# Gate and up of the last layer by Strassen's method, two batches at a time

## The chip, the core and the metric

The kernel runs on one core of a Trainium2 chip (trn2). The metric is the device time of one execution in microseconds (us). A program on this core has five instruction streams that run side by side and wait for each other by semaphores: TensorE (PE in the profile, its weight loads PEld), VectorE (DVE), ScalarE (ACT), GpSimd (POOL) and SyncE (SP), which here issues the loads and stores.

## The reference

Four sublayers on x of 4 batches x 512 tokens x 512 features, float32: attention over a context, a mixture of experts, a second attention, and a feed-forward layer, which alone is changed:

```python
x = fwht(x * SU_ug) / SCALE
x_up = x @ W_up.T * (Wscale_ug[:INTER] * SCALE)
x_gate = x @ W_gate.T * (Wscale_ug[INTER:] * SCALE)
x = jax.nn.silu(x_gate) * x_up
x = fwht(x * SU_dp) / SCALE
x = x @ W_down.T * (Wscale_dp * SCALE)
```

Its input is the layernorm of the running x, its output is added to it; INTER is 2048. fwht is a Hadamard transform over the last axis.

## The kernel before

A matrix product in this kernel is three: every operand is split into a high and a low part of TensorE's rounded fp32 type, ACT copying the high part and DVE subtracting it from the raw value, and `product` (L91) multiplies high by high, high by low and low by high into one PSUM bank. The last layer is `final_ffn` (L2887). The transforms of its hidden side are folded into the down weights ahead of it (`fold_dram`). It has 64 steps `s`, `divmod(s, NF)` being the batch b and the tile j of 128 of the 2048 hidden features. Per step, TensorE computes gate and up of the tile for the 512 tokens of the batch (`gate_up`, 2 x 4 x 3 matmuls of 512 columns), always one step ahead, and then `down`, 4 x 3 matmuls that add to four PSUM banks psY over the 16 tiles of a batch. ACT applies silu, DVE multiplies by up and its scale, casts the high part and subtracts for the low (`hidden`), and both split the next weights. After the last tile of a batch DVE adds the four banks to x (`add_y`) and SP stores it. The order of each stream is the one in which its loop is written.

The layer's input for the next batch is made beside that: DVE's statistics (`stats`, four rows at j = 1), GpSimd's `rstd`, then for each 128 tokens ACT's `row_norm`, GpSimd's `row_fly` (five instructions: the signs and two butterfly levels), TensorE's `turn_row` (transposes) and `rotate` (a product with a Hadamard matrix of 128), each result split by ACT and DVE. Turns and rotations are put between gate and up of the next step and the down product (`beside`), in banks that gate and up need two steps later. Loads of gate and up (512 KB) and down (256 KB) are three steps ahead, in slots of one buffer (`final_raw`).

## Time and profile before

| | us |
|---|---|
| median of 3 runs | 2234.42 |
| lowest and highest | 2230.71, 2235.13 |
| the profiled execution | 2232.4 |
| its span, first to last instruction | 2230.6 |
| busy in the span: PE, PEld | 2205.2, 1844.6 |
| DVE, ACT, POOL | 1436.4, 1043.1, 470.0 |

Busy times are those of one profiled execution, on the same scale as its span. A matmul's record reaches into the next one's, so busy PE time is that of overlapping records; what one takes from the stream is the distance of two starts. The mean granted clock of TensorE is 0.999 of full speed.

### The profile page before, as it was taken

To read this page: it belongs to the slowest core of one execution; us is meant where nothing else is said; L and a number is where in the kernel's file an instruction comes from. 1 tells how busy PE (TensorE), PEld (TensorE's weight loads), DVE (VectorE), ACT (ScalarE), POOL (GpSimd) and SP (SyncE) were. 2 spreads that over 40 slices of the span, in tenths; PEclk is the share of its full clock that TensorE was granted. 3 is DMA by queue.
4 is the path that set the end of the run, shared out by engine and by line. 5 is a ranking of instruction groups with operands and counts; after the bars stand their busy time and mean duration, and the time that the engine had idled before them with its cause. 6 is when DMAs were issued, how large, how long until landed. Compare 5 with 4: busy or idle time off the path is not lost. (4 is left out here: it accounts for less than half of the span.)

```text
span 2230.6 us, 32169 instructions
## 1 busy us (share of the span) xinstructions
PE 2205.2 (99%) x11065; PEld 1844.6 (83%) x11065; DVE 1436.4 (64%) x2993; ACT 1043.1 (47%) x1871; POOL 470.0 (21%) x445
## 2 busy tenths in 40 slices
PE   8999999999999999999999999999999999999999
PEld 6778788888999977888888888888878888888887
DVE  7864365546777766777777777777776555555544
ACT  5532220114556566666666666666664233223221
POOL 4432545521111171011000010000142102121000
PEclk9999999999999999999999999999999999999999
...
DMA packets 92171, 219.58 MB, mean 98 GB/s; under 512 B 9568, under 2 KB 30560, under 8 KB 89248
## 3 DMA queue, kind: packets, MB, share of 16 engines
...
q8 instruction: 65, 1.06, 0.2%
...
## 5 line engine op out<-in xcount | busy, mean ns | idle before, releaser
L2245 ACT ACTIVATE route_weights<-route_weights,xa_minus_max 128x512 f32<-128x512 f32 x256 | 184.7, 722 | 188.6 <-DVE xa_minus_max L2400 188.5
L2416 DVE TENSOR_TENSOR xa_late_hi<-xa_ps_t,route_wv_hi 128x512 fp32r<-128x512 f32 x256 | 174.8, 683 | 118.3 <-ACT route_wv_hi L2254 118.1
L2183 POOL TENSOR_TENSOR route_kv_lo<-route_rows,route_kv_hi 128x1024 fp32r<-128x1024 f32 x32 | 77.0, 2407 | 695.2 <-ACT route_kv_hi L2219 695.2
L2254 ACT ACTIVATE route_wv_hi<-xa_ps_t 128x512 fp32r<-128x512 f32 x256 | 151.1, 591 | 93.7 <-PE xa_ps_t L2606 66.7
L2400 DVE CUSTOM_DVE_ANT_0 route_weights<-xa_ps_s,route_mask_bias 128x512 f32<-128x512 f32 x256 | 175.5, 686 | 0.6 <-issue 0.6
L2992 ACT ACTIVATE ffn_silu<-ffn_ps_gate,late_scales 128x512 f32<-128x512 f32 x63 | 43.5, 690 | 244.7 <-PE ffn_ps_gate L96 244.7
L2606 PEld LDWEIGHTS xa_ps_t<-ident,route_weights 128*128 128x128 f32 x1024 | 126.5, 140 | 36.4 <-issue 3.8
L2606 PE MATMUL xa_ps_t<-ident,route_weights 128*128 128x128 f32 x1024 | 153.3, 272 | 1.9 <-DVE xa_late_hi L2416 1.8
L94 PE MATMUL xa_ps_p<-route_wv_hi,route_kv_hi 128*128 128x512 f32 x288 | 119.2, 414 | 3.0 <-PEq L1632 1.4
L2798 DVE TENSOR_TENSOR route_kv_lo<-route_weights,route_kv_hi 128x1024 fp32r<-128x1024 f32 x42 | 53.8, 1282 | 99.7 <-ACT route_kv_hi L2793 99.7
L1095 ACT ACTIVATE moe_silu<-moe_ps_gate 128x512 f32<-128x512 f32 x44 | 26.3, 597 | 190.3 <-PE moe_ps_gate L96 190.3
L94 PE MATMUL xa_ps_p<-late_xT_hi,late_wq_hi 128*128 128x512 f32 (+1 forms) x264 | 113.6, 430 | 0.2 <-DVE late_wq_lo L2798 0.2
L96 PE MATMUL xa_ps_p<-route_wv_hi,route_kv_lo 128*128 128x512 f32 x288 | 113.2, 393 | 0.0
L94 PE MATMUL xa_ps_s<-route_kv_hi,xa_q_hi 128*128 128x512 f32 x256 | 103.6, 405 | 0.7 <-DVE xa_minus_max L2400 0.7
L94 PE MATMUL xa_ps_o<-route_first_lo,xa_late_lo 128*128 128x512 f32 x256 | 103.5, 404 | 0.0
L96 PE MATMUL xa_ps_p<-late_xT_hi,late_wq_lo 128*128 128x512 f32 (+1 forms) x264 | 103.4, 392 | 0.0
L95 PE MATMUL xa_ps_p<-late_xT_lo,late_wq_hi 128*128 128x512 f32 (+1 forms) x264 | 102.6, 389 | 0.0
L2422 DVE TENSOR_TENSOR x<-xa_ps_o,x 128x512 f32<-128x512 f32 x126 | 86.1, 683 | 25.5 <-PE xa_ps_o L96 24.4
L94 PE MATMUL ex_ps_h<-ex_xT_hi,ex_w_hi 128*128 128x256 f32 (+1 forms) x360 | 101.9, 283 | 0.4 <-DVE ex_w_lo L1758 0.4
L96 PE MATMUL ex_ps_h<-ex_xT_hi,ex_w_lo 128*128 128x256 f32 (+1 forms) x360 | 101.1, 281 | 0.0
L96 PE MATMUL xa_ps_s<-route_kv_hi,xa_q_lo 128*128 128x512 f32 x256 | 100.7, 393 | 0.0
L94 PE MATMUL ffn_ps_y<-ffn_down_hi,ffn_hidden_hi 128*128 128x512 f32 x256 | 100.3, 392 | 0.0
...
## 6 DMA issues: line engine op xcount, KB each, us to landing
...
```

What stands on the lines that cost most here:

```text
L94: pe.matmul(out, lh, rh, start=start, stop=False)
L95: pe.matmul(out, lh, rl, start=False, stop=False)
L96: return pe.matmul(out, ll, rh, start=False, stop=stop)
L2183: pool.tensor_tensor(kvl[b % 2][:], rawkv[b % 2], f32(kvh[b % 2][:]), ALU.subtract).then_inc(M.kv_ready, 1)
L2245: act.activation(prob[slot][:], prob[slot][:], ACT.Exp, bias=nmx[:, slot:slot + 1], scale=-1.0, accum_out=tot[:, slot:slot + 1]).then_inc( ...
L2254: act.activation(PTh[:, :, tt * P:(tt + 1) * P], psT[tt % 2][:].rearrange("p (k n) -> p k n", k=TT), ACT.Copy).then_inc(M.pt_hi, 1)
L2400: dve.tensor_tensor_reduce(out=prob[slot][:], in0=psS[slot % 2][:], in1=maskb[:, b * S:(b + 1) * S], scale=-SCALE, scalar=3.4e38, op0=ALU. ...
L2416: dve.tensor_tensor(PTl[:, :, tt * P:(tt + 1) * P], psT[tt % 2][:].rearrange("p (k n) -> p k n", k=TT), f32(PTh[:, :, tt * P:(tt + 1) * P] ...
L2422: dve.tensor_tensor(x[:, t, :], psO[tt % 2][:], x[:, t, :], ALU.add).then_inc(M.x_added, 1)
L2606: last = pe.transpose(psT[tt % 2][:, k * P:(k + 1) * P], prob[tt][:, k * P:(k + 1) * P], ident)
L2798: dve.tensor_tensor(L.gu_lo[s % 3][:], final_raw(G, s)[0], f32(L.gu_hi[s % 3][:]), ALU.subtract).then_inc(L.gu_ready, 1)
L2992: act.activation(hid[s % 2][:], gate[:], ACT.Silu, scale=gate_s[:, j:j + 1]).then_inc(M.silu_done, 1)
```

## The change

Batches 0 and 1 form a pair, and 2 and 3. The gate and up weights of a tile are taken as a 2 x 2 matrix of blocks (gate or up by half of the 512 inputs), the inputs of a pair as another (half of the inputs by batch). Seven products of blocks, P1 to P7, replace eight; each block product is 2 x 3 matmuls. Their operands are sums of blocks: `weight_sums` makes those of the weights in place on GpSimd, for every tile anew, and DVE and ACT split them beside the plain weights; t1 to t4, of the inputs, are made once per pair of batches, t1 and t2 by DVE, t3 and t4 by GpSimd, from unsplit copies (`rot_copy`) that ACT writes beside the split ones. The products are added up in SBUF: five additions on DVE, two on GpSimd, copies of P1 and P5 on ACT. The first batch's hidden tile goes on to its down product as before; the second's is kept, unsplit, in one of seven places, and its down products are done in flushes after tiles 5, 10 and 15 (10 and 15 in the first pair), since psY holds one batch at a time; each change of batch adds psY to x. The first five tiles of the first pair are plain steps of batch 0, and later of batch 1, while the inputs of batch 1 are not all there. So there are 37 steps, 10 plain and 27 of pairs, and 64 down products. Transposes and rotations move to other steps; rotations come after the down product. Rows 4 and 5 and unsplit copies for batch 0 are made in the attention before. Gate and up weights have two split slots instead of three.

```diff
+PLAIN = 5
+KEPT = 7
+PAIR_BATCHES = ((0, 1), (2, 3))
+FLUSH = ((10, NF - 1), (5, 10, NF - 1))
...
+def final_steps():
+    steps = []
+    for p, (a, b) in enumerate(PAIR_BATCHES):
+        plain = 0 if p else PLAIN
+        steps += [Step("plain", p, j, a) for j in range(plain)]
+        kept = []
+        for j in range(plain, NF):
+            kept.append(len(steps))
+            steps.append(Step("pair", p, j, a))
+            if j in FLUSH[p] and not (plain and j == NF - 1):
+                steps[-1].tail, kept = kept, []
+        steps += [Step("plain", p, j, b) for j in range(plain)]
+        if kept:
+            steps[-1].tail = kept
+    return steps
...
-        NORM1, TURN1, NORM2, ROT1, TURN2, ROT2 = 2, 6, 7, 8, 10, 12
+        TURNS = {0: (4,), 1: (5,), 2: (6, 7), 15: (8, 9), 16: (10,), 17: (11,), 18: (12, 13), 19: (14,), 20: (15,)}
+        ROTATES = {1: 2, 2: 3, 17: 4, 18: 5, 19: 6, 20: 7}
+        NORMS = {1: (6,), 2: (7,), 9: (8,), 10: (9,), 16: (10, 11), 17: (12,), 18: (13,), 19: (14, 15)}
+        STATS = {6: 2, 8: 3}
...
+                def weight_sums(s):
+                    pool.wait_ge(L.gu_ready, splits_before(s) + 1)
+                    q = [final_raw(G, s)[0][:, i * 2 * P:(i + 1) * 2 * P] for i in range(4)]
+                    sums.link(pool.tensor_tensor(q[3], q[2], q[3], ALU.add))
+                    sums.link(pool.tensor_tensor(q[2], q[0], q[2], ALU.subtract))
+                    sums.link(pool.tensor_tensor(q[0], q[3], q[0], ALU.subtract))
+                    pool.tensor_tensor(q[1], q[1], q[0], ALU.subtract).then_inc(M.sums_taken, 1)
+                def t3(p):
+                    pool.wait_ge(M.t_odd, 2 * p + 1)
+                    if p == 0:
+                        pool.wait_ge(M.x_lo, x_count(p, "b1"))
+                    pool.tensor_tensor(X.raw_t3, X.raw_b[1], X.raw_b[0], ALU.subtract).then_inc(M.t_even, 1)
+                def t4(p):
+                    pool.wait_ge(M.t_odd, 2 * p + 2)
+                    pool.tensor_tensor(X.raw_t4, X.raw_a[1], X.raw_t2, ALU.subtract).then_inc(M.t_even, 1)
+                def add_p5(q):
+                    pool.wait_ge(M.p5_copied, q + 1)
+                    pool.wait_ge(M.added, added_count(q, "p1_p6"))
+                    if q:
+                        pool.wait_ge(M.kept_ready, q)
+                    pool.tensor_tensor(part[2], part[0], kept[q % KEPT], ALU.add).then_inc(M.p5_added, 1)
+                    pool.wait_ge(M.added, added_count(q, "p1_p6_p7"))
+                    pool.tensor_tensor(kept[q % KEPT], part[0], kept[q % KEPT], ALU.add).then_inc(M.p5_added, 1)
+                for s in range(NSTEPS):
+                    if is_pair(s + 1):
+                        weight_sums(s + 1)
+                    if is_pair(s):
+                        add_p5(STEPS[s].pairs)
+                    if s in (PLAIN - 1, LAST_PLAIN):
+                        t3(STEPS[s + 1].pair)
+                        t4(STEPS[s + 1].pair)
+                    if s in STATS:
+                        rstd(STATS[s])
+                    for t in NORMS.get(s, ()):
                         row_fly(pool, L, t)
 
...
+                    else:
+                        if opens:
+                            x_high(st.pair, "t3")
+                        split_gate_up(s + 1)
...
+                        act.wait_ge(M.product_done, product_count(q, "p5"))
+                        act.activation(kept[q % KEPT], bank_p5[:], ACT.Copy).then_inc(M.p5_copied, 1)
+                        if not (opens or followed):
+                            hidden_high(s - 1)
+                        act.wait_ge(M.product_done, product_count(q, "p1"))
+                        if opens:
+                            act.wait_ge(M.hidden_ready, s)
+                        act.activation(part[0], bank_p1[:], ACT.Copy).then_inc(M.p1_copied, 1)
+                        if not (opens and STEPS[s - 1].tail):
+                            split_down(STEPS[s - 1].event + 1)
+                        act.wait_ge(M.added, added_count(q, "gate_a"))
+                        silu(s, 1, part[1])
+                        if opens:
+                            x_high(st.pair, "t4")
+                        if tail:
+                            tail_high(s - 1, 0)
+                        split_sums(s + 1)
+                        act.wait_ge(M.added, added_count(q, "gate_b"))
+                        silu(s, 2, part[2])
+                        if tail:
+                            hidden_high(s)
+                        for e in range(len(tail)):
+                            split_down(STEPS[s - 1].event + 2 + e)
+                            tail_high(s - 1, e + 1)
+                    for t in NORMS.get(s, ()):
+                        row_norm(act, G, L, t)
...
+                def keep(s):
+                    j, q = STEPS[s].j, STEPS[s].pairs
+                    dve.wait_ge(M.silu_done, s + q + 2)
+                    dve.wait_ge(M.p5_added, 2 * q + 2)
+                    tile = kept[q % KEPT]
+                    dve.scalar_tensor_tensor(out=tile, in0=tile, scalar=up_s[:, j:j + 1], in1=part[2],
+                                             op0=ALU.mult, op1=ALU.mult).then_inc(M.kept_ready, 1)
+                def gate_a(q):
+                    dve.wait_ge(M.product_done, product_count(q, "p2"))
+                    dve.wait_ge(M.p1_copied, q + 1)
+                    dve.wait_ge(M.hidden_ready, pair_step(q))
+                    dve.tensor_tensor(part[1], bank_p2[:], part[0], ALU.add).then_inc(M.added, 1)
...
+                def seventh(q):
+                    dve.wait_ge(M.product_done, product_count(q, "p7"))
+                    dve.wait_ge(M.p5_added, 2 * q + 1)
+                    dve.tensor_tensor(part[0], bank_p7[:], part[0], ALU.add).then_inc(M.added, 1)
...
+                def up_a(q):
+                    dve.wait_ge(M.step_done, pair_step(q) + 1)
+                    dve.wait_ge(M.p5_added, 2 * q + 2)
+                    dve.tensor_tensor(part[0], bank_p4[:], part[0], ALU.add).then_inc(M.added, 1)
...
+                    else:
+                        if opens:
+                            x_low(st.pair, "t3")
+                        split_gate_up(s + 1)
+                        gate_a(q)
+                        sixth(q)
+                        if not (opens and STEPS[s - 1].tail):
+                            split_down(STEPS[s - 1].event + 1)
+                        seventh(q)
+                        if opens:
+                            x_low(st.pair, "t4")
+                        if tail:
+                            tail_low(s - 1, 0)
+                            add_y(STEPS[s - 1].event)
                         else:
+                            split_sums(s + 1)
+                            if opens:
+                                add_y(STEPS[s].event - 1)
+                        gate_b(q)
+                        up_a(q)
+                        hidden(s, 1, part[0])
+                        for e in range(len(tail)):
+                            split_down(STEPS[s - 1].event + 2 + e)
+                            tail_low(s - 1, e + 1)
+                            if e == 0:
+                                split_sums(s + 1)
+                        if tail:
+                            add_y(st.event - 1)
+                    if s in STATS:
+                        for t in range(STATS[s] * TT, STATS[s] * TT + TT):
                             stats(t)
...
+                add_y(STEPS[-1].event)
+                split_down(STEPS[-1].event + 1)
+                for e in range(len(STEPS[-1].tail)):
+                    tail_low(NSTEPS - 1, e)
+                    split_down(STEPS[-1].event + 2 + e)
...
+                def pair_up(s, between):
+                    st = STEPS[s]
+                    q, p = st.pairs, st.pair
+                    w, sums = (L.gu_hi[s % 2], L.gu_lo[s % 2]), (sum_hi[s % 2], sum_lo[s % 2])
+                    opens = not is_pair(s - 1)
+                    pe.wait_ge(L.gu_ready, splits_before(s) + 2)
+                    if opens:
+                        pe.wait_ge(M.prod_done, s - 1)
+                        pe.wait_ge(M.x_lo, x_count(p, "t1"))
+                    else:
+                        pe.wait_ge(M.p5_copied, q)
+                        pe.wait_ge(M.added, added_count(q - 1, "p1_p6_p7"))
+                    times(bank_p5, sums, 3, X.t1).then_inc(M.product_done, 1)
+                    times(bank_p1, w, 0, X.a[0]).then_inc(M.product_done, 1)
+                    if opens:
+                        pe.wait_ge(M.silu_done, s + q)
+                    else:
+                        pe.wait_ge(M.added, added_count(q - 1, "gate_b"))
+                    times(bank_p2, w, 1, X.a[1]).then_inc(M.product_done, 1)
+                    if opens:
+                        pe.wait_ge(M.prod_done, s)
+                        pe.wait_ge(M.x_lo, x_count(p, "t2"))
+                    else:
+                        pe.wait_ge(M.added, added_count(q - 1, "up_a"))
+                    times(bank_p6, sums, 0, X.t2).then_inc(M.product_done, 1)
+                    between(range(TT // 2))
+                    if opens:
+                        pe.wait_ge(M.x_lo, x_count(p, "t3"))
+                    pe.wait_ge(M.p1_copied, q + 1)
+                    times(bank_p7, sums, 2, X.t3).then_inc(M.product_done, 1)
+                    between(range(TT // 2, TT))
+                    pe.wait_ge(M.added, added_count(q, "gate_a"))
+                    times(bank_p3, sums, 1, X.b[1]).then_inc(M.product_done, 1)
+                    if opens:
+                        pe.wait_ge(M.x_lo, x_count(p, "t4"))
+                    pe.wait_ge(M.added, added_count(q, "p1_p6"))
+                    times(bank_p4, w, 3, X.t4).then_inc(M.step_done, 1)
...
+                for s, st in enumerate(STEPS):
+                    if s == LAST_PLAIN:
+                        turns(s)
+                        down_step(s)
+                        rotates(s)
+                        for r in st.tail[:-1]:
+                            down_kept(r)
+                        pair_up(s + 1, lambda tiles: down_kept(st.tail[-1], tiles))
+                    elif is_pair(s + 1):
+                        pair_up(s + 1, lambda tiles: down_step(s, tiles))
+                        for r in st.tail:
+                            down_kept(r)
```

In the order of the instructions, VectorE first: one step of a tile before (`ffn_silu` is the hidden tile, `route_kv` and `late_wq` the gate and up weights), and one pair step of the change (`ffn_part` are sums of products, `ffn_sums` the weight sums, `route_rows` here a kept tile). The semaphores in brackets bear names of earlier sublayers, whose numbers they reuse.

```order
L2798 TENSOR_TENSOR late_wq_lo<-route_weights,late_wq_hi 128x1024 [waits late_gate_up_hi]
L3041 SCALAR_TENSOR_TENSOR ffn_silu1<-ffn_ps_up1,late_scales,ffn_silu1 128x512 [waits ca_x_loaded0,ca_x_loaded1]
L3046 CAST ffn_hidden_hi1<-ffn_silu1 128x512 [waits ca_ln_xT_ready]
L3048 TENSOR_TENSOR ffn_hidden_lo1<-ffn_silu1,ffn_hidden_hi1 128x512 [waits ca_ln_hi_ready]
L3014 TENSOR_TENSOR ffn_down_lo2<-route_weights,ffn_down_hi2 128x512 [waits ca_ctx_loaded0]
```

```order
L2897 TENSOR_TENSOR route_kv_lo0<-route_weights,route_kv_hi0 128x1024 [waits late_gate_up_hi]
L3417 TENSOR_TENSOR ffn_part1<-ffn_ps_gate0,ffn_part0 128x512 [waits ca_ln_pool_chain,ca_ln_chain,ca_ln_stats_done]
L3423 TENSOR_TENSOR ffn_part0<-ffn_ps_up0,ffn_part0 128x512 [waits moe_table_taken,ca_ln_stats_done]
L3333 TENSOR_TENSOR ffn_down_lo2<-route_weights,ffn_down_hi2 128x512 [waits ca_x_loaded3]
L3429 TENSOR_TENSOR ffn_part0<-ffn_ps_up1,ffn_part0 128x512 [waits moe_table_summed,ca_ln_stats_done]
L3343 TENSOR_TENSOR route_kv_lo1<-route_weights,route_kv_hi1 128x1024 [waits late_gate_up_hi]
L3434 TENSOR_TENSOR route_wv_room_5188<-ffn_ps_gate0,route_wv_room_5188 128x512 [waits moe_table_summed,ca_ln_stats_done]
L3439 TENSOR_TENSOR ffn_part0<-ffn_ps_up0,ffn_part0 128x512 [waits moe_table_summed,ca_ln_hi_ready]
L3392 SCALAR_TENSOR_TENSOR ffn_part1<-ffn_part0,late_scales,ffn_part1 128x512 [waits ca_ln_xn_turned,moe_table_taken]
L3410 SCALAR_TENSOR_TENSOR route_rows<-route_rows,late_scales,route_wv_room_5188 128x512 [waits moe_table_summed,ca_ln_xn_turned]
L3402 TENSOR_TENSOR ffn_hidden_lo0<-ffn_part1,ffn_hidden_hi0 128x512 [waits ca_ln_rstd_ready]
```

Five instructions for one tile of one batch have become eleven for one tile of two.

GpSimd, which before has nothing in a step but, at some, the rows of the next batch (no row of it names a weight or a product): its part of a pair step, the four sums of weights and the two additions of a product.

```order
L3146 TENSOR_TENSOR route_weights<-route_weights 128x256 [waits late_gate_up_ready]
L3147 TENSOR_TENSOR route_weights<-route_weights 128x256 [waits ca_x_loaded0]
L3148 TENSOR_TENSOR route_weights<-route_weights 128x256 [waits ca_x_loaded0]
L3149 TENSOR_TENSOR route_weights<-route_weights 128x256 [waits ca_x_loaded0]
L3168 TENSOR_TENSOR route_wv_room_5188<-ffn_part0,route_rows 128x512 [waits moe_hot_ready,moe_table_taken,ca_first]
L3170 TENSOR_TENSOR route_rows<-ffn_part0,route_rows 128x512 [waits moe_table_taken]
```

The sums wait for VectorE's split of the plain weights, which they overwrite; the additions wait for VectorE's and VectorE's next for them.

VectorE in the step after tile 10 of the first pair, where batch 1's kept tiles are multiplied: after the addition of P7, from the split of the first kept tile to that of the second (`route_first_lo` and `mask_room` take the split tiles).

```order
L3367 TENSOR_TENSOR route_first_lo<-route_rows,route_first_lo 128x512 [waits moe_counts_ready]
L3378 TENSOR_TENSOR x<-ffn_ps_y0,x 128x512 [waits moe_routed]
L3378 TENSOR_TENSOR x<-ffn_ps_y1,x 128x512 [waits moe_routed]
L3378 TENSOR_TENSOR x<-ffn_ps_y2,x 128x512 [waits moe_routed]
L3378 TENSOR_TENSOR x<-ffn_ps_y3,x 128x512 [waits moe_counted]
L3434 TENSOR_TENSOR route_wv_room_5188<-ffn_ps_gate0,route_wv_room_5188 128x512 [waits moe_table_summed,ca_ln_stats_done]
L3439 TENSOR_TENSOR ffn_part0<-ffn_ps_up0,ffn_part0 128x512 [waits moe_table_summed,ca_ln_hi_ready]
L3392 SCALAR_TENSOR_TENSOR ffn_part1<-ffn_part0,late_scales,ffn_part1 128x512 [waits ca_ln_xn_turned,moe_table_taken]
L3410 SCALAR_TENSOR_TENSOR route_wv_room_5188<-route_wv_room_5188,late_scales 128x512 [waits moe_table_summed,ca_ln_xn_turned]
L3402 TENSOR_TENSOR ffn_hidden_lo1<-ffn_part1,ffn_hidden_hi1 128x512 [waits ca_ln_rstd_ready]
L3333 TENSOR_TENSOR ffn_down_lo0<-route_weights,ffn_down_hi0 128x512 [waits ca_x_loaded3]
L3367 TENSOR_TENSOR mask_room_5187<-route_rows,mask_room_5187 128x512 [waits moe_counts_ready]
```

Four additions to x and the rest of the pair step now stand between the split of the first kept tile and that of the second.

## Rows read from the trace of the kernel before

**Rows 1.** The page: busy time, share of the span and instructions
```profile
PE 2205.2 (99%) x11065; PEld 1844.6 (83%) x11065; DVE 1436.4 (64%) x2993; ACT 1043.1 (47%) x1871; POOL 470.0 (21%) x445
```

**Rows 2.** Waits of PE from 1690 us: total, times, longest
```profile
PE ffn_ps_up L94 <- PEq L2119: 0.6, 1, 0.6
```

**Rows 3.** Stretches of the last layer: length, busy by engine, PEclk, DMA share, GB/s
```profile
1965.00:2096.00 131.00, 131.00 (x595) 108.95 (x594) 74.27 (x100) 39.15 (x57) 23.54 (x24) 1.00 0.30 100
2096.00:2227.00 131.00, 131.00 (x579) 108.48 (x578) 58.86 (x84) 32.05 (x45) 0.00 (x0) 1.00 0.25 81
```

**Rows 4.** Timeline of PE and ACT: start, length, engine, line, operation
```profile
1992.29 0.39 PE L94 MATMUL ffn_ps_gate<-late_xT_hi,late_wq_hi 128*128 128x512 f32 x1
...
1997.73 0.39 PE L94 MATMUL ffn_ps_y<-ffn_down_hi,ffn_hidden_hi 128*128 128x512 f32 x1
...
2210.73 0.39 PE L96 MATMUL ffn_ps_gate<-late_xT_hi,route_kv_lo 128*128 128x512 f32 x1
...
2211.15 0.69 ACT L2992 ACTIVATE ffn_silu<-ffn_ps_gate,late_scales 128x512 f32<-128x512 f32 x1 [6.00 <-PE ffn_ps_gate L96]
```

**Rows 5.** Timeline of DVE while POOL is idle
```profile
1821.74 1.23 DVE L2798 TENSOR_TENSOR route_kv_lo<-route_weights,route_kv_hi 128x1024 fp32r<-128x1024 f32 x1 [4.48 <-ACT route_kv_hi L2793]
1822.89 0.75 DVE L3041 SCALAR_TENSOR_TENSOR ffn_silu<-ffn_ps_up,late_scales,ffn_silu 128x512 f32<-128x512 f32 x1
1823.67 0.43 DVE L3046 CAST ffn_hidden_hi<-ffn_silu 128x512 fp32r<-128x512 f32 x1
1824.13 0.69 DVE L3048 TENSOR_TENSOR ffn_hidden_lo<-ffn_silu,ffn_hidden_hi 128x512 fp32r<-128x512 f32 x1
1824.74 0.69 DVE L3014 TENSOR_TENSOR ffn_down_lo<-route_weights,ffn_down_hi 128x512 fp32r<-128x512 f32 x1
```

**Rows 6.** Timeline of DVE at the end
```profile
2225.43 2.73 DVE L3035 TENSOR_TENSOR x<-ffn_ps_y,x 128x512 f32<-128x512 f32 x4 [1.46 <-PE ffn_ps_y L96]
```

**Rows 7.** Groups of ACT from 1700 us: busy, mean ns, idle before
```profile
L2992 ACT ACTIVATE ffn_silu<-ffn_ps_gate,late_scales 128x512 f32<-128x512 f32 x63 | 43.5, 690 | 244.7 <-PE ffn_ps_gate L96 244.7
L2793 ACT ACTIVATE route_kv_hi<-route_weights 128x1024 fp32r<-128x1024 f32 x41 | 43.3, 1055 | 1.4 <-DMA route_weights<-in_ffn_w 1.4
L2982 ACT ACTIVATE ffn_down_hi<-route_weights 128x512 fp32r<-128x512 f32 x63 | 39.4, 625 | 0.0
```

**Rows 8.** Timeline of DVE, then POOL, around a row of the next batch
```profile
1762.45 1.76 DVE L2798 TENSOR_TENSOR route_kv_lo<-route_weights,route_kv_hi 128x1024 fp32r<-128x1024 f32 x1
1764.13 0.74 DVE L3041 SCALAR_TENSOR_TENSOR ffn_silu<-ffn_ps_up,late_scales,ffn_silu 128x512 f32<-128x512 f32 x1
1764.90 1.55 DVE L3046 CAST ffn_hidden_hi<-ffn_silu 128x512 fp32r<-128x512 f32 x1
...
1764.89 1.29 POOL L2817 TENSOR_TENSOR late_rows<-late_rows 128x512 f32<-128x512 f32 x1
1766.26 0.80 POOL L2821 TENSOR_TENSOR late_rows<-late_rows 128x256 f32<-128x256 f32 x1
...
1768.28 0.74 POOL L2821 TENSOR_TENSOR late_rows<-late_rows 128x256 f32<-128x256 f32 x1
```

**Rows 9.** Groups of POOL from 1600 us
```profile
L2821 POOL TENSOR_TENSOR late_rows<-late_rows 128x256 f32<-128x256 f32 x32 | 28.8, 900 | 2.5
...
L2183 POOL TENSOR_TENSOR route_kv_lo<-route_rows,route_kv_hi 128x1024 fp32r<-128x1024 f32 x2 | 4.8, 2410 | 24.0 <-ACT route_kv_hi L2219 24.0
```

**Rows 10.** Timeline of DVE, then POOL: statistics of one batch
```profile
1841.66 0.69 DVE L152 BATCH_NORM_STATS2 late_ln_stats<-x 128x6 f32<-128x512 f32 x1
...
1844.76 0.18 DVE L154 BATCH_NORM_AGGREGATE late_ln_mean_var<-late_ln_stats 128x2 f32<-128x6 f32 x1
...
1845.11 0.23 POOL L135 TENSOR_SCALAR late_ln_var_eps<-late_ln_mean_var 128x4 f32<-128x4 f32 x1 [75.39 <-DVE late_ln_mean_var L154]
...
1847.60 0.24 POOL L140 TENSOR_SCALAR late_ln_shift<-late_ln_shift 128x4 f32<-128x4 f32 x1
```

**Rows 11.** Waits of PE over the whole span, the longest in total
```profile
PE xa_ps_t L182 <- DVE late_xT_lo L171: 2.6, 2, 2.0
```

589 lines of the change are left out of this document (430 added, 159 removed).

## The prediction

> **What bounds the kernel now.** I read the shares of busy time first, then the waits of TensorE in the last layer, then the durations of what stands in its loops. TensorE (PE) is busy 99% of the span [rows 1]. From 1690 us to the end it waited once, 0.6 us at the start of the stage [rows 2], and in the stretches from 1965 to 2227 us it is busy all the time at clock 1.00, while VectorE (DVE) has 74 and 59 of each 131 us and GpSimd (POOL) 24 and 0 [rows 3]. So the last layer is as long as its matmuls. A removed matmul is worth its pitch, not its listed 0.39 us, since records overlap: the 24 of one gate and up start at 1992.29 and the next product at 1997.73 [rows 4], 5.44 / 24 = **0.2267 us**. Six take 1.36, twelve 2.72. A result is seen by others 0.19 us after its pitch ends: last start 2210.73, ScalarE (ACT) starts at 2211.15 [rows 4].
>
> The excerpts of the order show the method in force: a step for a pair of tiles has seven block products of six matmuls instead of eight. 27 pairs save 27 x 6 = 162 matmuls, **36.7 us**. The down products stay. Everything else in the change either lies beside TensorE or makes it wait; all of the prediction is in how long it waits, since now it never does.
>
> **Prices.** DVE with both inputs in SBUF: 1.23 us for 128x1024, 0.69 for 128x512 (back to back 1.15 and 0.61 apart) [rows 5]. The multiplication by the scale takes 0.75 [rows 5], an addition of a product from PSUM 2.73 / 4 = 0.68 [rows 6]. ACT: 1.06 for 1024 columns, 0.62 for 512, silu 0.69 [rows 7]. GpSimd: 0.74 for 256 columns and 0.08 to the next that needs it, 1.29 for 512 [rows 8], 2.41 for 1024 [rows 9].
>
> **Two engines that shut each other out.** In [rows 8] GpSimd's row work runs beside DVE's splits. The cast that takes 0.43 alone [rows 5] takes 1.55: GpSimd started 0.01 us before it and ran 1.29, to 1766.18, and 1.29 + 0.43 is about what is seen, a wait to the end of the other's instruction. A split of 1.23 takes 1.76 there. The multiplication in between, one input of which is in PSUM, takes 0.74 as ever. So I count: of the new DVE work, what has both inputs in SBUF takes turns with GpSimd, instruction by instruction; what reads a product from PSUM doesn't. The Trainium skill, SBUF — State Buffer (on the ports shared by VectorE and GpSimd), calls it an exclusive lock held for a whole instruction. [...]
>
> **The loop of a pair step.** TensorE's own time is (42 + 12) x 0.2267 = 12.24. Let T be the start of P5. The first order excerpt lists DVE's eleven instructions, the second GpSimd's six. In the steady state the sums are ready at T. Then GpSimd's second addition (1.29, after DVE's split of the sums) T+1.3; up_a T+2.0; the product of the first batch T+2.75; that kept for the second T+3.5; hidden_lo (ACT's hi beside it) T+4.2; the split of the next gate and up T+5.4; GpSimd's four sums 4 x 0.82 = 3.3, with DVE's split of down (0.6) in between, T+9.4; its first addition T+10.7; DVE's seventh T+11.4 and the split of the sums, T+12.7. So the loop is about **12.75**: TensorE waits 0.5 per step once no slack is left. Slack comes where TensorE is late for another reason: then hidden_lo ends at T+3.1 (P4, 0.19, up_a, 0.75, 0.75, 0.69), and three steps pass free. Over both halves I count 3.6 us of such waits (0 if the loop is 12.0; 12 if it is 13.2).
>
> **What is put into that loop has no cover.**
> - Statistics of batches 2 and 3, at steps 6 and 8: 3.3 us on DVE (from 1841.66 to 1844.94) and 2.7 on GpSimd before the next sums [rows 10], of which 1.8 count behind the split: next sums at T+17, 4.8 late. Twice: **9.6** (6 to 11).
> - Rows 8 and 9 on GpSimd at steps 9 and 10: 1.29 + 4 x 0.74 + gaps = 4.4, taking turns with four DVE instructions. Sums at T+16.6, 4.4 late; the other one falls in a flush and makes it 4.0 longer: **8.4** (0 to 10).
> - Flush inside a run of pairs, three times (third order excerpt). The second kept tile needs from DVE, from T+10.7 on: seventh, a split, four additions to x, gate_b, up_a, two products, hidden_lo, a split of down, a split: thirteen instructions, 9.1 us, T+19.8. TensorE is there at T+12.24+2.72 = 14.96, so it waits 4.85. 3 x 4.85 = **14.6** (9 to 17; 3 each if seventh is not held up by GpSimd).
> - The end: after the last P4 nothing is left to cover up_a, the product, ACT's hi and hidden_lo: 0.19 + 0.68 + 0.75 + 0.62 + 0.69 and gaps, 3.15. Then the first kept tile is split only behind four additions to x that wait for the last down product: 2.25. **5.4** (4 to 7). The finish behind it, the additions to x [rows 6] and the stores, stays.
>
> **Openings.** Let C be the end of gate and up of step 3. The rotation of batch 1's last rows is copied at C+5.2. Then in DVE's order: t1 1.2, three splits 3.6, gate and up 1.2 (C+11.2); GpSimd's sums 3.9, ACT 1.06, and DVE waits for GpSimd's 2.4 of t3 to end before its split: C+18.7. TensorE, after gate and up of step 4 and a down product, stands from C+13.4: 5.3. Behind it t2, hidden of step 4 (its cast waits for GpSimd's t4) and the split of t2 end at C+24.7, P6 waits 1.9; t4 makes P4 wait 2.7 and the next sums 1.1. **11.0** (6 to 14; 5.6 without turns). The second opening, after step 20, is alike but with five kept tiles in between: GpSimd has rows 14 and 15 (8.8 us from about 4.6 before the end of gate and up of step 20) ahead of the sums; ACT's split of these stands ahead of row 15's; the rotation waits 4.7 and row 15 1.0; t3 holds the second kept tile back 3.1; x4, the sums and the additions to x behind them cost 1.3 + 1.2 + 2.6. **14** (6 to 18).
>
> **Rotations.** At steps 1, 2, 17 and 18 they now come after the down product, into the bank that gate and up of the step after next needs at once: TensorE waits 0.9 for two ACT copies (0.19 + 0.62 + the rest of the first). **3.6** (2 to 6). The copies and rows moved ahead into the attention are on ACT and GpSimd, whose waits there end with TensorE; 0, up to 2 if that cover is gone. The additions to x grow from 16 to 40; those in the flush are in the sum, the others lie beside kept products. Loads keep their bytes, 768 KB each 8 us before, and less each step now: 0.
>
> **Sum.** Waits 3.6 + 9.6 + 8.4 + 14.6 + 5.4 + 11.0 + 14 + 3.6 = 70.2; less 36.7 is +33.5. The profiled execution took 2232.4 (span 2230.6), 2.0 under the median of 2234.4. 2232.4 + 33.5 = **2266**, and its own range, with errors of a few us in each wait, 2250 to 2282.
>
> **Rivals.**
> 1. *The loop fits (faster).* Place: the sums' split against the next P5. If the engines did not take turns, the loop loses 0.6 + 1.2 and is 10.9; if DVE's order also leaves room for statistics, rows and second opening, only rotations 3.6, first opening 5.6, flush 3 x 3 and end 5.4 remain, 23.6: 2232.4 - 36.7 + 23.6 = **2219**. It decides when all waits are under 36.7. For it: DVE's own work in a step is 8.4 of 12.24 us, GpSimd's 5.9. Against: they are in one chain, and the stretched rows [rows 8]. 0.12.
> 2. *No turns, but the chain as I have it.* Statistics 6.2 and second opening 6 on top: 35.8 of waits, **2231.5**, no change to be told. 0.12, half of it within 0.2%.
> 3. *Waits that cost more.* GpSimd's in-place sums at the 0.90 mean of [rows 9] instead of 0.74 make the loop 0.6 longer, some 9 us over about 15 steps without slack. Or the clock: no wait in this kernel is over 2.0 us [rows 11] and the clock of the last layer stays 1.00 [rows 3]; here nine are over 3. At the lower level, 1.2 GHz, a block product is 1.36 longer; one after each wait is 12.2. **2278**. The Trainium skill, TensorE: Matmul & The Clock Gate (on the gate), says that an idle engine is put to half rate and comes back after sustained work; no row here shows it. 0.14.
>
> The forecast has 0.62. A measurement of this kernel can tell 0.2%, 4.5 us, from no change. Faster: 0.12 + 0.02; same: 0.06; slower: 0.62 + 0.14 + 0.04 = 0.80. The range reaches from rival 2 to past rival 3: 2231 to 2286 leaves out rival 1 and a little above.
>
> **What would show it.** 2142 matmuls of 512 columns in the last layer; PE busy well under all of the time between 1704 us and the end. The longest waits: P5 of steps 5, 8, 10 and 11 for DVE's split of the sums; a down product for the split of a kept tile in three flushes, 4 to 9 us; the rotation of step 20. DVE's SBUF splits over their 1.23 and 0.69 in the mean, the additions from PSUM at 0.68. It is wrong if P5 to P5 is 12.3 in plain pair steps with the sums ready well ahead, if the splits are not stretched, or if GpSimd's additions end before P7 does.

## The result and the profile after

The changed kernel takes **2282.5 us** in the median of 4 runs (2280.8 to 2284.3), the kernel before, on the same chip, 2233.3 (2230.7 to 2235.1). The ratio is **1.022, interval 1.021 to 1.024: slower**. The profiled execution took 2282.8 with a span of 2281.0 us, 50.4 more than the 2230.6 of before. The forecast was 2266 with a range to 2286, so direction and range held; the place of half of the loss did not.

Shares of busy time and the granted clock in 40 slices of the changed kernel:

```profile
PE 2195.0 (96%) x10903; PEld 1826.5 (80%) x10903; DVE 1522.1 (67%) x3103; ACT 1125.6 (49%) x1996; POOL 660.1 (29%) x611
...
PEclk9999999999999999999999999999999999999999
```

Against [rows 1], TensorE has 162 matmuls less and is busy 10 us less, not 36.7: part of the busy time is matmuls at a lower clock. The row of PEclk shows nothing at one digit; the mean granted clock of the span is 0.988 against 0.999.

TensorE's waits from 1690 us (us in total, times, longest), where the kernel before had the one of [rows 2]:

```profile
PE ffn_ps_up L94 <- PEq L2122: 12.9, 1, 12.9
PE ffn_ps_gate L94 <- DVE ffn_sums_lo L3343: 8.9, 4, 4.0
PE ffn_ps_y L94 <- DVE route_first_lo L3367: 7.7, 3, 2.9
PE ffn_ps_gate L94 <- DVE route_kv_lo L3343: 6.4, 3, 4.3
PE ffn_ps_gate L2931 <- POOL late_rows L2922: 3.4, 1, 3.4
PE ffn_ps_y L94 <- DVE ffn_hidden_lo L3402: 3.4, 2, 3.0
...
PE ffn_ps_y L94 <- DVE x L3378: 2.9, 1, 2.9
```

One line was not in the forecast at all: 12.9 us for "PEq", TensorE's own sequencer. It is the boundary between the block of the attention and that of the last layer. Timelines there, of TensorE, GpSimd and ScalarE:

```profile
1697.71 0.39 PE L96 MATMUL xa_ps_o<-route_first_lo,xa_late_lo 128*128 128x512 f32 x1
1710.98 0.77 PE L94 MATMUL ffn_ps_up<-late_xT_hi,late_wq_hi 128*128 128x512 f32 x1 [12.88 <-PEq L2122]
...
1697.44 0.24 POOL L140 TENSOR_SCALAR late_ln_shift<-late_ln_shift 128x4 f32<-128x4 f32 x1
1698.61 1.26 POOL L2916 TENSOR_TENSOR late_rows<-late_rows 128x512 f32<-128x512 f32 x1 [0.93 <-ACT late_rows L2904]
...
1706.41 0.72 POOL L2922 TENSOR_TENSOR late_rows<-late_rows 128x256 f32<-128x256 f32 x1
...
1697.71 1.52 ACT L2904 ACTIVATE late_rows<-x,late_ln_shift,late_ln_rstd 128x512 f32<-128x512 f32 x2 [6.12 <-POOL late_ln_shift L140]
1710.65 0.63 ACT L3192 ACTIVATE ffn_down_hi<-route_weights 128x512 fp32r<-128x512 f32 x1 [11.42 <-PEq L2122]
```

TensorE's last product of the attention starts at 1697.71. GpSimd then still has rows 4 and 5 ahead of it, ten instructions to 1707.13, and no engine passes into the next block before it: ScalarE starts there at 1710.65, TensorE at 1710.98.

The rest of the waits, 45.8 us in 26 places, lie where the forecast had put them, mostly smaller. And the clock, in stretches of 20 us (length, busy and matmuls of TensorE, granted clock, DMA share, GB/s):

```profile
1710.00:1730.00 20.00, 19.02 (x75) 0.85 0.44 158
1750.00:1770.00 20.00, 15.69 (x62) 0.91 0.14 41
...
1790.00:1810.00 20.00, 15.98 (x65) 0.91 0.19 64
1830.00:1850.00 20.00, 15.71 (x61) 0.91 0.15 52
...
2130.00:2150.00 20.00, 20.00 (x90) 1.00 0.23 59
```

and the two us behind the wait for P5 of step 8, first as such a stretch, then in the timeline of TensorE, a block product of six:

```profile
1806.00:1808.00 2.00, 2.00 (x6) 0.50 0.60 195
...
1805.45 0.80 PE L94 MATMUL ffn_ps_gate<-late_xT_hi,ffn_sums_hi 128*128 128x512 f32 x1 [4.02 <-DVE ffn_sums_lo L3343]
1806.04 0.63 PE L95 MATMUL ffn_ps_gate<-late_xT_lo,ffn_sums_hi 128*128 128x512 f32 x1
1806.47 0.63 PE L96 MATMUL ffn_ps_gate<-late_xT_hi,ffn_sums_lo 128*128 128x512 f32 x1
...
1807.75 0.63 PE L96 MATMUL ffn_ps_gate<-late_xT_hi,ffn_sums_lo 128*128 128x512 f32 x1
1808.17 0.47 PE L94 MATMUL ffn_ps_up<-late_xT_hi,late_wq_hi 128*128 128x512 f32 x1
1808.48 0.40 PE L95 MATMUL ffn_ps_up<-late_xT_lo,late_wq_hi 128*128 128x512 f32 x1
```

Between 1806.04 and 1807.75 the matmuls start 0.43 us apart, at a granted clock of 0.50, which is 1.2 GHz; from 1808.48 they are back at the 0.2267 of [rows 4]. [Rows 3] had no stretch under 1.00.

**Where 50.4 us come from.** I went through TensorE's timeline from start to start of its records and counted what lies over 0.2267 us a record. Behind the boundary that is 72.4 us more than in the same stage of the kernel before: 45.8 of listed waits; 15.6 in 78 matmuls that start 0.40 to 0.43 apart; and 11.0 in what stands beside the waits, since the record before a wait and the first one behind it last longer, about 0.4 us together. The boundary costs 12.25 more than before (from last start to first start 13.27, before 1.02), and the attention ended 2.4 later in this execution. 72.4 + 12.25 + 2.4 - 36.7 = 50.4.

### The profile page after: what moved, and what is told of

Read it like the earlier page. It is cut to its first block and busy times, and to the rows that moved or that the text cites. A ratio compares the mean times of both kernels' runs of the same rounds, so it can differ in the third digit from the quotient of the medians.

```text
span 2281.0 us, 32353 instructions
## 1 busy us (share of the span) xinstructions
PE 2195.0 (96%) x10903; PEld 1826.5 (80%) x10903; DVE 1522.1 (67%) x3103; ACT 1125.6 (49%) x1996; POOL 660.1 (29%) x611
## 5 line engine op out<-in xcount | busy, mean ns | idle before, releaser
L1545 POOL DMA_INDIRECT route_rows<-moe_xn,route_slot_token x39 | 44.4, 1137 | 239.4 <-PE ex_ps_t L1837 182.8
L94 PE MATMUL xa_ps_o<-route_first_lo,xa_late_lo 128*128 128x512 f32 x256 | 103.8, 406 | 0.0
L96 PE MATMUL xa_ps_o<-route_first_lo,xa_late_lo 128*128 128x512 f32 x256 | 100.4, 392 | 0.0
L95 PE MATMUL xa_ps_p<-xa_late_hi,route_kv_hi 128*128 128x512 f32 x256 | 100.1, 391 | 0.0
```

What stands on the lines that cost most here:

```text
L94: pe.matmul(out, lh, rh, start=start, stop=False)
L95: pe.matmul(out, lh, rl, start=False, stop=False)
L96: return pe.matmul(out, ll, rh, start=False, stop=stop)
L1545: pool.indirect_dma_start(out=G.rows[:, at:at + C], out_offset=None, in_=G.xn_dram, in_offset=bass.IndirectOffsetOnAxis(ap=G.slot_token[:, ...
```

## The experiments

Every comparison is with runs of the kernel before on the same chip. A "span" is that of the profiled execution, a sum of waits that of TensorE's listed waits from 1690 us: 0.6 before, **58.7** in the changed kernel. Where I give a gain over the changed kernel in us, it is a difference of two medians taken on different chips; the kernel before had 2233.3 beside the changed kernel and 2233.5 to 2236.0 beside the runs below, so such a gain is uncertain by up to 3 us, and the ratios are the safer numbers. The length of the last layer, from TensorE's first matmul in it to the end of the span, is free of that: 534.3 us before, 570.0 in the changed kernel.

### Is the saving real? One block product in eight left out

```diff
-                        for k in range(KC):
+                        ks = KC // 2 if o and (b == 1 and j >= 5 or b == 3) else KC
+                        for k in range(ks):
```

The kernel *before*, in which up leaves out half of its inner dimension for 27 pairs: as many matmuls less as the seven products, and nothing else. The output lacks that part.

> The kernel before, with one block product in eight left out for 27 of the 32 pairs of tiles (of up, the second half of the inputs for batch 1 from tile 5 on and for batch 3): 162 matmuls of 512 columns fewer, everything else as it was. It leaves out part of the up product. Theory: the 36.7 us (162 x 0.2267) that the prediction counts as saved are there to be had when nothing else gets in the way: 2233.3 - 36.7 = 2196.6, give or take 2. Rival: VectorE's or ScalarE's work per tile is a bound too close behind, then it is over 2205.

Measured: 2199.5 us (2198.2 to 2200.3) against 2235.2, ratio 0.984 [0.982, 0.986], and one wait of 0.6 us. **35.7 of the 36.7 us are there** when nothing else changes.

### The block boundary: rows 4 and 5 behind it

```diff
@@ GpSimd, end of the attention @@
-                row_fly(pool, L, TT)
-                row_fly(pool, L, TT + 1)
@@ GpSimd, start of the last layer @@
+                row_fly(pool, L, TT)
+                row_fly(pool, L, TT + 1)
                 for s in range(NSTEPS):
```

ScalarE's two row_norm move alike.

> The change, but the rows 4 and 5 (ScalarE's two row_norm, GpSimd's two row_fly) stand at the start of the last layer's block and no longer at the end of the attention's. Theory: in the changed kernel TensorE stands 12.9 us at the boundary of the two blocks because GpSimd finishes these rows there (its last row instruction ends at 1707.13, TensorE had nothing after 1697.71), and its first 12 matmuls then run at half the clock. So the wait falls to about the 0.6 of the kernel before, and about 2.4 us of slow matmuls go with it: 2282.5 - 12.3 - 2.4 = 2268, give or take 2. Rival: the boundary itself has become slower (3.85 us pass between the end of GpSimd's last row and TensorE's first matmul), then 3 to 4 us of the wait stay and it is 2272; or the rows come back as waits of the first transposes, and it stays at 2280.

Measured: 2276.3 (2271.3 to 2278.8), ratio 1.019 [1.017, 1.021], span 2269.5. TensorE's first matmuls of the last layer:

```profile
1699.77 0.47 PE L94 MATMUL ffn_ps_up<-late_xT_hi,late_wq_hi 128*128 128x512 f32 x1 [2.89 <-PEq L2122]
1700.08 0.40 PE L95 MATMUL ffn_ps_up<-late_xT_lo,late_wq_hi 128*128 128x512 f32 x1
1700.31 0.40 PE L96 MATMUL ffn_ps_up<-late_xT_hi,late_wq_lo 128*128 128x512 f32 x1
```

The wait falls from 12.88 to 2.89, and the stage starts at full clock (0.23 apart). The 0.6 that my theory expected is not reached; the 2.89 that stay are close to the rival's 3 to 4. 1.9 us come back where gate and up of step 2 now wait for row 4. The median gains 6.2 us. The span gains 11.5, of which 1.2 are an earlier end of the attention; the profiled execution is the fastest of the four, by 5 us. What is left of the boundary is GpSimd's again: its last instruction ends at 1696.47 and ScalarE passes at 1699.42.

### Statistics and rows away from the pair loop

```diff
-        NORMS = {1: (6,), 2: (7,), 9: (8,), 10: (9,), 16: (10, 11), 17: (12,), 18: (13,), 19: (14, 15)}
-        STATS = {6: 2, 8: 3}
+        NORMS = {1: (6,), 2: (7,), 14: (8,), 15: (9,), 16: (10, 11), 17: (12,), 18: (13,), 19: (14, 15)}
+        STATS = {11: 2, 15: 3}
+        RSTD = {11: 2, 16: 3}
```

VectorE takes the statistics of batch 2 in the flush, ahead of the last additions to x.

> The change, but the statistics of batch 2 stand in VectorE's idle time at the end of the flush after tile 10 (step 11), those of batch 3 after step 15, and rows 8 and 9 at steps 14 and 15 (before: statistics at 6 and 8, rows at 9 and 10). Theory: the waits of P5 in steps 8 (4.02), 10 (3.77) and 11 (1.29) and 1.7 in the flush after tile 10 are these four pieces of work in the chain between VectorE and GpSimd; they go, 10.8 us, and with them the stretches at half clock behind two or three of them, another 4 to 8: 2264 to 2268. Rival: the chain itself is too long, then the waits come back spread over the steps as 0.5 each and it is 2275 or more.

Measured: 2275.1 (2274.4 to 2277.0), ratio 1.018 [1.016, 1.020]. The waits of 4.02, 3.77 and 1.29 at P5 of steps 8, 10 and 11 are gone, and the first flush's fall from 4.63 to 2.89. But TensorE's timeline has a longer one where gate and up of step 17 wait for the turned rows:

```profile
1936.14 0.77 PE L94 MATMUL ffn_ps_gate<-late_xT_hi,route_kv_hi 128*128 128x512 f32 x1 [4.92 <-DVE late_xT_lo L2954]
```

It was 2.10 before this move: the statistics of batch 3 now stand ahead of the rows' low parts on VectorE. I had expected 14 to 18 us less and got 7.4; the rest was given back at this next chain and in slow matmuls, of which there still are 71. The time is the rival's, its mechanism is not: no wait came back spread over the steps.

### Kept tiles split earlier in the flush

```diff
                         if tail:
                             tail_low(s - 1, 0)
                             add_y(STEPS[s - 1].event)
+                            for e in range(2):
+                                split_down(STEPS[s - 1].event + 2 + e)
+                                tail_low(s - 1, e + 1)
```

ScalarE's order is changed alike, and the loop behind the hidden tile starts at the third.

> The change, but in each of the three flushes inside a run of pairs ScalarE and VectorE split the second and third kept tiles and their down weights directly behind the four additions to x, ahead of the rest of the pair step. Theory: the waits for the second kept tile (2.9 three times, and 1.7) are thirteen VectorE instructions in line; with seven of them moved behind, some 1 us of the 2.9 is left and 1 to 2 for the fourth kept tile: 3 to 7 us less by the waits, and up to 1.7 each by the clock: 2271 to 2279. Rival: the wait is held by GpSimd's addition ahead of seventh, not by what stands behind, then nothing changes, 2282.

Measured: 2272.6 (2272.2 to 2274.8), ratio 1.017 [1.015, 1.019]. The waits for the second kept tile fall from 2.88 to 0.65 twice and from 1.70 to 0.64; the 2.93 for the first stays (2.89). That is 5.5 us of waits and 9.9 of time. 5.8 more are clock, with 49 matmuls at 0.40 to 0.43 apart instead of 78. Against that stand 2.5 us at the rotation and the kept tile behind row 15 (3.08 and 2.58 for 1.83 and 1.33), which other runs without any edit there show too.

### The weight sums left out

```diff
                     pool.wait_ge(L.gu_ready, splits_before(s) + 1)
...
-                    sums.link(pool.tensor_tensor(q[0], q[3], q[0], ALU.subtract))
-                    pool.tensor_tensor(q[1], q[1], q[0], ALU.subtract).then_inc(M.sums_taken, 1)
+                    pool.sem_inc(M.sums_taken, 1)
```

> The changed kernel with GpSimd's four weight sums of each pair step left out (the raw weights go through in their place, so the sums of the block products are not the reference's). Theory (the sums are paid only where they stand in a late chain, in the openings and behind the statistics, and the steady pair loop hides them): the waits of 4.31, 4.02, 3.77 and 1.29 us at steps 5, 8, 10 and 11 shrink to under 1 us each and take their clock with them, the rest of the waits (block boundary 12.9, flushes, rows and rotations, end) stays, and the time is 2262 to 2268. Rival (VectorE and GpSimd in turns on one way into the memory slow the whole pair loop): the steps between the waits get shorter too, by 0.3 us or more in each of 27, and the time falls below 2256. By VectorE's groups: the split of the sums falls from 1383 ns to 1290, the split of the down weights from 719 to under 700.

Measured: 2255.4 (2252.9 to 2257.5), ratio 1.010 [1.008, 1.011]. Waits are down to 42.8, matmuls at 0.40 to 0.46 to 33. Below my range, and just past the bound that I had given the rival, but not by its mechanism: the steps between the waits were at TensorE's own pace already (see the loop below) and could not get shorter. The 28.6 us between the two spans are 15.8 of waits, 9.0 of slow matmuls, 3.5 of what stands beside the waits and 0.2 of the attention's end. My error was to count only the chains at steps 5 to 11; the flushes (2.88 to 1.56 twice, 4.6 to 3.3 in the first) and the small waits of the second opening hang on the sums too. The 13 splits of the sums that are listed as `ffn_sums_lo` stayed at 1385 ns in the mean, and the other 14, listed as `route_kv_lo`, went from 1291 to 1329, so it is not the sums that stretch them. GpSimd's second addition is what runs beside them (see the loop below); no run takes it away. The split of down fell from 719 to 698.

### Matmuls that nobody reads, in the waits: two attempts

```diff
                     else:
                         pe.wait_ge(M.p5_copied, q)
+                    fill(bank_p5, w, FILL.get(s, 0))
+                    if not opens:
                         pe.wait_ge(M.added, added_count(q - 1, "p1_p6_p7"))
+                    pe.wait_ge(L.gu_ready, splits_before(s) + 2)
```

This is the second attempt, with FILL = {5: 17, 8: 15, 10: 14}: n matmuls into the bank of P5, and only behind them the wait for the additions and the one for the split of the sums. In the first, fill stood behind the wait for the additions.

> The changed kernel with 46 matmuls more, whose result nobody reads, put into the three waits before the first block product of steps 5, 8 and 10 (17, 15 and 14 of them, 0.2267 us each, in place of waits of 4.31, 4.02 and 3.77 us): the chain that the waits stand for is untouched, only TensorE is no longer idle in it. Theory (the clock falls because TensorE idles, and costs a few us behind each long wait): no wait is left at the three places but a few tenths, the slices behind them (1760, 1800, 1820 us) stand at full clock, and the time falls by 4 to 7 us, to about 2277. Rival (the lower clock has nothing to do with the waits, or the records after them only look longer): 2282 as before, or 1 us more, and the slices stay at 0.91.

Measured: 2285.8 (2283.2 to 2290.4), ratio 1.024 [1.022, 1.025]. Only step 5 was a test. At steps 8 and 10 the fill itself waited 2.89 and 2.73 us for the bank and then ran in part at the lower clock:

```profile
1803.22 5.10 PE L3561 MATMUL ffn_ps_gate<-late_wq_hi 128*128 128x512 f32 x15 [2.89 <-DVE ffn_part L3429]
```

5.10 us for 15, 0.34 each: it took longer than the wait it was to fill. So the second attempt:

> The changed kernel with the same 46 unread matmuls as in the first such run, but at steps 8 and 10 ahead of the wait for the additions to the bank of the first block product (there TensorE had stood idle 2.89 and 2.73 us before the first of them, and they ran at 0.34 us each): now TensorE has work through the whole of each of the three waits. Theory (idling lowers the clock, work keeps it): no wait over 0.6 us before P5 of steps 5, 8 and 10, the three slices behind them at a granted clock of 1.00 instead of 0.91, and the time 4 to 7 us below the changed kernel, 2276 to 2279. Rival (the slices at 0.91 come from something else): they stay, and the time is 2282 or more.

Measured: 2283.9 (2280.8 to 2288.0), ratio 1.023 [1.021, 1.024]. Of the stretches of TensorE:

```profile
1750.00:1770.00 20.00, 18.02 (x78) 1.00 0.15 45
1790.00:1810.00 20.00, 19.33 (x86) 1.00 0.14 40
1830.00:1850.00 20.00, 16.16 (x70) 1.00 0.14 40
1850.00:1870.00 20.00, 15.65 (x61) 0.91 0.04 14
```

The theory of the clock holds: with work in the waits (0.52, 0.67, 0.98 left) the three stretches stand at 1.00 instead of 0.91. The time does not follow. From the first matmul of the last layer to P5 of step 10 it is 123.2 us against 124.3, and the next wait is longer instead:

```profile
1848.46 0.47 PE L94 MATMUL ffn_ps_gate<-late_xT_hi,route_kv_hi 128*128 128x512 f32 x1 [2.86 <-DVE route_kv_lo L3343]
```

It was 1.29. What TensorE gains at full clock behind a late chain it gives back at the next one, as VectorE and GpSimd set the time there. The 1.1 us are still there at the end of the profiled execution (its last layer takes 568.9 us, the changed kernel's 570.0), which is less than medians of four runs can tell. So not all of the 15.6 us in slow matmuls were to be had.

### All moves together, three versions

The arithmetic is that of the changed kernel; orders and tables differ, and from the second version on one rounding is on another engine. The first version joins the moves of the runs above with those that its expectation names; of the new ones:

```diff
-        TURNS = {0: (4,), 1: (5,), 2: (6, 7), 15: (8, 9), 16: (10,), 17: (11,), 18: (12, 13), 19: (14,), 20: (15,)}
-        ROTATES = {1: 2, 2: 3, 17: 4, 18: 5, 19: 6, 20: 7}
+        TURNS = {0: (4,), 1: (5,), 2: (6, 7), 15: (8, 9), 16: (10,), 17: (11, 12), 18: (13,), 19: (14, 15)}
+        ROTATES = {1: 2, 2: 3, 16: 4, 17: 5, 18: 6, 19: 7}
@@ VectorE, plain step @@
+                        beside(s - 1)
                         if s:
                             add_y(STEPS[s - 1].event)
-                        beside(s - 1)
                         if s == PLAIN - 2:
+                            split_gate_up(s + 2)
@@ TensorE, ahead of gate (i = 0) and up (i = 1) @@
-                        pe.wait_ge(L.copied, 2 * ROTATES[s] + 2)
+                        pe.wait_ge(L.copied, 2 * ROTATES[s] + i + 1)
```

> All scheduling moves together, the arithmetic of the changed kernel untouched: rows 4 and 5 behind the block boundary and their statistics ahead of the last additions of the attention; statistics of batches 2 and 3 in VectorE's gaps of the first flush, rows and rotations one step earlier; second and third kept tile split ahead of the hidden tile in each flush, the first kept tile of the end ahead of the last one; the split of step 5's gate and up a step earlier; turned rows taken before the additions to x; gate and up wait for one rotation bank each. Theory (the seven products save about 36 us, and all of the loss is waits at single places with the clock behind them): the waits from 1690 us on fall from 58.5 to 12 to 20 us and the mean clock rises to 0.995 or more, so 2230.6 - 36.7 + 16 + 5 = 2215, in 2208 to 2225, below the kernel before. Rival (waits only move to the next late chain, as with the statistics alone): 2235 to 2255.

Measured: 2243.0 (2237.2 to 2244.4) against 2233.5, ratio 1.004 [1.003, 1.006], span 2235.3; waits 31.7, mean clock 0.998. It keeps 39.5 us of the loss from happening, but the time is in the rival's range, not in the theory's: 31.7 us of waits were left where I had expected 12 to 20, most of them at new places. The profiled execution, whose waits and clock these are, was the fastest of five; the others took 2240.7 to 2244.4 at a clock of 0.994 to 0.996.

Second version: statistics behind the fourth kept tile, rows normalised ahead of the rotation copies, beside(s - 1) ahead of hidden(s) on VectorE, the rounding of step 4's hidden tile on ScalarE.

> The scheduling moves of the run before (31.7 us of waits left, span 2235.3), with its remaining late chains put earlier: the statistics of batches 2 and 3 behind the fourth kept tile of the first flush instead of ahead of it (wait of 3.03); rows 8 and 9 a step earlier and rows 10 to 15 normalised ahead of the rotation copies (waits of 1.94, 0.59, 1.21, 3.19); the turned rows taken by VectorE before the hidden tile of the step (2.67); the rounding of step 4's hidden tile on ScalarE instead of VectorE (openings of 1.65, 1.49, 1.92). Theory (every loss is such a place, and what is left is the saving of the seven products): waits from 1690 us on fall to 12 to 18 us and the span to 2217 to 2224, a median of 2220 to 2228, faster than the kernel before by 0.3 to 0.6%. Rival (VectorE and GpSimd are by now so full that a wait moved comes back): the waits stay at 25 us or more and the time at 2232 or more.

Measured: 2231.6 (2229.0 to 2237.0, 11 runs) against 2235.0, ratio 0.999 [0.998, 1.000]; waits 23.2. That lies between the theory (to 18 us of waits, 2228) and the rival (from 25, 2232). The 2.67 and all four waits for rows (1.94, 0.59, 1.21, 3.19) are gone, but rows 8 and 9, a step earlier, hold up the sums of step 14 (2.41), six statistics ahead of the last kept tile are too many (2.58), and P5 of step 5 went up, from 1.65 to 3.22, since VectorE's split of that step's gate and up now came behind two turned rows and GpSimd's sums with it.

Third version: that split ahead of the turned rows, rows 8 and 9 back, and

```diff
-        STATS = {11: {4: (8, 9, 10, 11, 12, 13), 5: (14, 15)}}
+        STATS = {11: {3: (8,), 4: (9, 10, 11), 5: (12, 13, 14, 15)}}
@@ VectorE, pair step @@
-                        seventh(q)
                         if opens:
                             x_low(st.pair, "t4")
+                        seventh(q)
```

(the numbers in front are places in the first flush); the sums of step 21 are split behind the second kept tile.

> The run before (23.2 us of waits left, span 2229.7) with four more late chains put earlier: VectorE splits step 5's gate and up ahead of the turned rows, so that GpSimd's sums start about 3.5 us earlier (wait of 3.22); the low part of t4 ahead of the seventh product's addition (1.62); of the statistics of batches 2 and 3 four ahead of the last kept tile of the first flush and four behind it (2.58), and rows 8 and 9 back where they did not delay the sums (2.41, for which 1.9 comes back); the sums of step 21 split behind the second kept tile (1.33, 1.47). Theory (each wait that goes is time that goes): the waits from 1690 us on fall to 12 to 15 us, and the median is 8 to 13 us below the 2231.6 of the run before, 2219 to 2224, faster than the kernel before by 0.5 to 0.7%. Rival (at this level the waits are no longer what sets the time, or they only move): 2228 or more.

Measured: **2224.3** (2221.6 to 2225.8) against 2236.0, ratio **0.994 [0.993, 0.996]**: faster than both kernels. TensorE's waits in it (total, times, longest):

```profile
PE ffn_ps_y L94 <- DVE ffn_hidden_lo L3417: 3.4, 2, 3.0
PE ffn_ps_y L94 <- DVE mask_room L3382: 2.7, 3, 1.5
PE ffn_ps_up L2928 <- POOL late_rows L2919: 1.9, 1, 1.9
...
PE ffn_ps_up L94 <- PEq L2122: 1.2, 1, 1.2
```

17.5 us of waits in 21 places, the longest the 2.96 of the end, for which I tried nothing; I had expected 12 to 15. By the count of start to start, what lies behind the boundary is 25.9 us more than in the kernel before, against 72.4. Three versions, the same arithmetic: 31.7, 23.2 and 17.5 us of waits, 2243.0, 2231.6 and 2224.3 us. In the profiled executions the last layer takes 538.7, 529.0 and 523.5 us, 534.3 in the kernel before: from the first version to the third 15.2 us for 14.2 of waits.

## Why the prediction was right, and where it was wrong

| step of the prediction | said | measured |
|---|---|---|
| 162 matmuls less | -36.7 | -35.7, alone |
| copies and rows moved ahead into the attention | 0, up to 2 | 12.25 |
| steady loop | 3.6 | 0 |
| statistics | 9.6 | 7.8 (4.02, 3.77) |
| rows 8 and 9 | 8.4 | 1.3 |
| flushes | 14.6 | 10.4 |
| first opening (with 0.2 for a row) | 11.0 | 6.9 |
| second opening | 14 | 11.3 |
| rotations | 3.6 | 3.2 (4 x 0.79) |
| end | 5.4 | 4.9 |
| clock, and what stands beside the waits | only in rival 3, 12.2 | 26.6 (15.6, 11.0) |

**Right** is the mechanism: a stage in which TensorE never waited gets chains without cover at single places. The places are the announced ones, the longest P5 of steps 5, 8 and 10 for the split of the sums. Statistics and rows 8 and 9 were moved in one run and lie one behind the other, so their two rows of the table can be told apart only in sum: 9.1 of 18.0.

**The failed step** is "The copies and rows moved ahead into the attention are on ACT and GpSimd, whose waits there end with TensorE; 0, up to 2 if that cover is gone". It looked for who waits for whom by semaphores. But the four operations on the statistics of batch 1 and row_fly of rows 4 and 5 stand last in GpSimd's program of that block, after VectorE's last statistics, and no engine starts the next block before they end. They run from 1695.73 to 1707.13; TensorE's last record ends at 1698.10, so 9.0 us of them have no cover. The remaining 3.2 are the boundary itself, which comes 3.5 us behind GpSimd's last operation and had come 0.3 behind TensorE's. I had priced a row at 4.4 us for rows 8 and 9; two of them, and 2.0 for the statistics, less the 2.4 that TensorE still covers, belonged in the sum. The run with the rows behind the boundary shows it: 12.88 becomes 2.89.

**The loop.** The prediction called itself wrong if P5 to P5 is 12.3 in plain steps with the sums ready well ahead. On this point it is. The starts of three P5 of the changed kernel, then VectorE and GpSimd in the second of these steps:

```profile
2124.30 0.39 PE L94 MATMUL ffn_ps_gate<-late_xT_hi,ffn_sums_hi 128*128 128x512 f32 x1
...
2136.54 0.39 PE L94 MATMUL ffn_ps_gate<-late_xT_hi,route_kv_hi 128*128 128x512 f32 x1
...
2148.78 0.39 PE L94 MATMUL ffn_ps_gate<-late_xT_hi,ffn_sums_hi 128*128 128x512 f32 x1
...
2139.31 0.69 DVE L3402 TENSOR_TENSOR ffn_hidden_lo<-ffn_part,ffn_hidden_hi 128x512 fp32r<-128x512 f32 x1 [0.43 <-ACT ffn_hidden_hi L3243]
2139.92 1.22 DVE L2897 TENSOR_TENSOR late_wq_lo<-route_weights,late_wq_hi 128x1024 fp32r<-128x1024 f32 x1
...
2146.23 0.69 DVE L3429 TENSOR_TENSOR ffn_part<-ffn_ps_up,ffn_part 128x512 f32<-128x512 f32 x1 [2.77 <-POOL route_wv_room L3168]
2146.84 1.22 DVE L3343 TENSOR_TENSOR ffn_sums_lo<-route_weights,ffn_sums_hi 128x1024 fp32r<-128x1024 f32 x1
...
2141.21 0.74 POOL L3146 TENSOR_TENSOR route_weights<-route_weights 128x256 f32<-128x256 f32 x1 [5.58 <-DVE late_wq_lo L2897]
...
2142.86 1.20 POOL L3148 TENSOR_TENSOR route_weights<-route_weights 128x256 f32<-128x256 f32 x1
...
2144.83 1.30 POOL L3168 TENSOR_TENSOR route_wv_room<-ffn_part,route_wv_room 128x512 f32<-128x512 f32 x1
2147.00 2.20 POOL L3170 TENSOR_TENSOR route_wv_room<-ffn_part,route_wv_room 128x512 f32<-128x512 f32 x1 [0.87 <-DVE ffn_part L3429]
...
2147.97 0.68 DVE L3434 TENSOR_TENSOR route_wv_room<-ffn_ps_gate,route_wv_room 128x512 f32<-128x512 f32 x1
```

The steps are 12.24 long, and the sums are ready at 2148.06, 0.7 ahead. I had set hidden_lo at T+4.2 and it ends at T+3.5: GpSimd's second addition begins ahead of the next P5, not behind the split of the sums, and is over at T+0.4 instead of T+1.3. From there the chain runs as written, and the four sums, one of them at 1.20, take 3.7 with what lies between. 12.75 became 11.5, which fits under TensorE's time. I take that mis-sized slack also for the reason why rows, flushes and openings came out shorter; no run tests it.

**The turns** hold: the second addition takes 2.20 instead of 1.29 where VectorE's split of 1.22 started 0.16 us before it, and gate_b (L3434), a sum with one input in PSUM, takes 0.68 in the midst of that addition; in the 17 of its 27 runs that lie wholly beside GpSimd's work its mean is 0.68, in the 7 that lie clear of it too. (Seventh can't tell, since it never runs beside GpSimd.) The Trainium skill, SBUF — State Buffer, Who interferes with whom, has a VectorE instruction with two inputs in SBUF contend with a GpSimd instruction that reads SBUF; the trace agrees with the first row. So the second rival, no turns, is out by its mechanism. The first, that the loop fits, had that half right, in spite of the turns; it is out by the other waits.

**The clock** was rival 3 and is real. The rate halves behind long waits, as the rows at 1806.04 show. The Trainium skill, TensorE: Matmul & The Clock Gate, on the gate, says that an idle engine is put to half rate, and the trace agrees at ten places. Its size here is 78 matmuls, 15.6 us, more than the nine block products (12.2) I had allowed: the ten places have 5 to 13 slow matmuls each instead of six, and one of them, with 11, is the boundary. I gave it 0.14 because no row of before showed it; the waits that I was forecasting were of a kind this kernel never had. The other part of rival 3, slower sums on GpSimd (3.3 us for four), did not come: 0.74 each where nothing shuts them out.

**Why the number was near.** Waits inside the stage 24.4 too many; boundary 12.3, clock and what stands beside the waits 26.6 and a later end of the attention 2.4 too few. (TensorE's last start in the attention moved without any edit to it, from 1696.5 to 1698.9 in six kernels with the changed one's attention, 1695.3 and 1698.6 in two with that of before.) The net is 16.9, and the span came out 16.9 over 2230.6 + 33.5 = 2264.1. That is luck in part: two errors of 24 and 41 us, of opposite sign, under a result within 17.

**Open.** How much of the 15.6 us of slow matmuls is cost and how much is absorbed by the next wait is known for three places only. The late start of step 5's sums, of rows and statistics could each be placed better still; the 2.96 of the end was left as it is.
